# A hybrid layer kernel on one core: four edits of order, at its head, in the first steps of its mixer and at the mixer's end

## The reference, cut to what matters

```python
def _layernorm(x, axis=-1, eps=1e-05):
    m = jnp.mean(x, axis=axis, keepdims=True)
    v = jnp.var(x, axis=axis, keepdims=True)
    return (x - m) / jnp.sqrt(v + eps)

x = x + (block-masked linear layer 512 -> 512 with bias)(_layernorm(x))
x = x + ffn(_layernorm(x))      # 4-bit weights with group scales, 512 -> 1792 -> 512
x = x + mixer(_layernorm(x))
x = x + ffn(_layernorm(x))      # the same weights again

# the mixer (a selective state space layer; 128 heads of 64 channels, chunks of 128 tokens)
proj = hidden_states @ in_proj_w.T            # gate z, then x, B, C (8 groups of 128), then dt
hBC = silu(causal depthwise convolution with 4 taps of [x, B, C] + conv_b)
dt = softplus(dt + dt_bias); A_dt = -exp(A_log) * dt
Y_diag = einsum('bclsh,bcshp->bclhp', (C B^T) * exp(segment sums of A_dt), x * dt)
Y_off  = einsum('bclhn,bchpn->bclhp', C, carried states) * exp(cumulated A_dt)
y = Y_diag + Y_off + D * x
y = y * rsqrt(mean(y^2) + eps) * norm_w * silu(gate)
return y @ out_proj_w.T
```

## Time and profile before

| | |
|---|---|
| median of 3 runs | 2114.71 us (2114.70 to 2115.32) |
| the profiled execution: its time | 2115.85 us |
| the profiled execution: its span in the trace | 2114.1 us |
| busy: PE, DVE, ACT, POOL | 2067.3, 1656.5, 1424.1, 887.6 us |
| DMA, share of 16 engines | 44.4% |

### The profile page before, as it was taken

How to read it: one execution, slowest core, us unless ns; L and a number is a source line. 1 busy time by engine, 2 the same in 40 slices (tenths; PEclk the granted TensorE clock), 3 DMA queues, 4 the chain that set the end, 5 groups by cost and what they waited for, 6 DMA issues and landing times.

```text
span 2114.1 us, 35693 instructions
## 1 busy us (share of the span) xinstructions
PE 2067.3 (98%) x12366; PEld 1703.4 (81%) x12366; DVE 1656.5 (78%) x2676; ACT 1424.1 (67%) x2690; POOL 887.6 (42%) x616
## 2 busy tenths in 40 slices
PE   7999998999999999999999999999999999989999
PEld 6788876788888888888888888888888888878887
DVE  7655557888888888888888888888888888876554
ACT  4322268878787878778787877877877878742221
POOL 1221214445454545454454544454545555422121
PEclk9999999999999999999999999999999999999999
DMA  5543225445444444444444444445444444455341
GB/s 204 176 139 136 78 85 184 151 140 158 147 138 154 139 154 148 150 160 133 142 156 150 144 155 134 150 154 162 139 155 140 154 149 145 148 172 172 131 147 40
DMA packets 160095, 307.06 MB, mean 145 GB/s; under 512 B 14528, under 2 KB 47552, under 8 KB 159680
## 3 DMA queue, kind: packets, MB, share of 16 engines
q1 hardware_dynamic: 159936, 305.00, 44.4%
HBM read 299.70 MB, written 5.24 MB: 144 GB/s over the span
## 4 chain that ended last, share of the span: by engine, by line
PE 78%; DVE 10%; issue 5%; ACT 4%; POOL 1%; DMA 1%; DVEq 0%; ACTq 0%; SPq 0%; POOLq 0%
PE ring L1016 30%; PE ring L1104 14%; PE bank L410 6%; PE bank_e L410 6%; PE yt L1085 5%; PE st L1069 4%; PE bank_e L422 3%; PE yt L1091 3%; PE bank L422 3%; PE xt L1056 3%; DVE xc L1458 1%; DVE ce L1511 1%; DVE em L1519 1%; DVE ygs L1538 1%; DVE bc L1458 1%
## 5 line engine op out<-in xcount | busy, mean ns | idle before, releaser
L1016 PE MATMUL ring<-m_lnt,w_sb 128*128 128x512 f32 x3456 | 858.9, 398 | 5.5 <-ACT sz L1265 2.5
L1016 PEld LDWEIGHTS ring<-m_lnt,w_sb 128*128 128x128 f32 x3456 | 630.1, 188 | 134.0 <-issue 3.1
L1688 POOL TENSOR_TENSOR w_sb<-w_raw,w_sb 128x512 fp32r<-128x512 f32 x288 | 428.4, 1490 | 162.3 <-ACT w_sb L1243 162.0
L1705 POOL TENSOR_TENSOR ysq<-ysq,y 128x512 f32<-128x512 f32 x126 | 169.8, 1348 | 637.2 <-ACT y L1299 637.2
L1104 PE MATMUL ring<-wo,ygs 128*128 128x512 f32 x1536 | 372.2, 392 | 5.6 <-DVE ygs L1538 3.3
L1104 PEld LDWEIGHTS ring<-wo,ygs 128*128 128x128 f32 x1536 | 289.2, 189 | 68.0 <-issue 7.8
L1458 DVE SCALAR_TENSOR_TENSOR xc<-ring,cw,xc 128x511 f32<-128x511 f32 (+2 forms) x384 | 286.8, 747 | 52.3 <-ACT xc L1255 43.2
L1285 ACT ACTIVATE cum_b<-cum_b,cum_q 128x128 f32<-128x128 f32 x1024 | 312.5, 390 | 0.0
L1243 ACT ACTIVATE w_sb<-w_raw 128x512 fp32r<-128x512 f32 x288 | 178.2, 620 | 48.0 <-DMA w_raw<-w_in 47.8
L1693 POOL TENSOR_TENSOR wo<-wo_raw,wo 128x512 fp32r<-128x512 f32 x128 | 191.1, 1493 | 1.6 <-ACT wo L1311 1.6
L1085 PE MATMUL yt<-em,x_dt 128*64 128x128 f32 x2048 | 183.9, 279 | 3.6 <-DVE state L1499 3.5
(11 more groups left out here) (198 smaller groups left out, 2891.9 us busy)
## 6 DMA issues: line engine op xcount, KB each, us to landing
w_raw<-w_in SPq DMA_DIRECT2D x288, 256.0 KB, 3.4
cum_b<-c_t SPq DMA_DIRECT2D x128, 512.0 KB, 4.6
ce<-e_t SPq DMA_DIRECT2D x128, 384.0 KB, 4.5
wo_raw<-w_out SPq DMA_DIRECT2D x128, 256.0 KB, 3.0
f_gu_q<-gu_w SPq DMA_DIRECT2D x28, 512.0 KB, 3.5
f_gu_zr<-gu_z SPq DMA_DIRECT2D x28, 512.0 KB, 4.3
f_gu_sr<-gu_s SPq DMA_DIRECT2D x28, 512.0 KB, 5.3
f_dn_q<-dn_w SPq DMA_DIRECT2D x28, 256.0 KB, 3.4
```

The costliest lines, as they stand in the source:

```text
L1016: mm = nc.tensor.matmul(dst[:], w_sb[:, u % WR, wp, k * P:(k + 1) * P], lnt[:, xp, k, b * S:(b + 1) * S], start=(i == 0), stop=(i == 3 * K ...
L1688: nc.gpsimd.tensor_tensor(w_sb[:, u % WR, 1], w_raw[:, u % NR], w_sb[:, u % WR, 0].bitcast(F32), ALU.subtract).then_inc(w_lo, 1)
```

## The change

The rows of instructions below are those of the built programs; names are the program's tiles, and a row's x2 or x4 counts equal instructions in a row. Line numbers behind L1096 are higher in the changed kernel (by 4 to 9).

The fourth edit is on PE, at `project_out(31, 0)`: its first nine matmuls (pairs 124 to 126) wait for 127 low parts of the gated output and of the output weights, and the last three for all 128. The whole diff:

```diff
--- before.py
+++ after.py
@@ -611,8 +611,8 @@
                 nc.scalar.activation(share[:], ones[:], ACT.Copy, scale=1.0 / P).then_inc(self.hi, 1)
                 norm_root(act, na, 0)
                 center(na, 0)
+                norm_root(act, na, 1)
                 high(na, 0)
-                norm_root(act, na, 1)
                 center(na, 1)
                 high_w(0)
                 high_w(1)
@@ -1097,10 +1097,14 @@
                 def project_out(i, t):
                     dst = ring_bank(("out", (i, t)))
                     ring_free(("out", (i, t)))
-                    pe.wait_ge(yg_lo, HALF * (i + 1))
-                    pe.wait_ge(wo_lo, HALF * (i + 1))
+                    early = 1 if (i, t) == (K // HALF - 1, 0) else 0
+                    pe.wait_ge(yg_lo, HALF * (i + 1) - early)
+                    pe.wait_ge(wo_lo, HALF * (i + 1) - early)
                     for m, (j, (yp, wp)) in enumerate((j, ab) for j in range(HALF * i, HALF * (i + 1))
                                                       for ab in PASSES):
+                        if early and m == 3 * (HALF - 1):
+                            pe.wait_ge(yg_lo, K)
+                            pe.wait_ge(wo_lo, K)
                         mm = nc.tensor.matmul(dst[:], ygs[:, j % OR, yp, t * P:(t + 1) * P], wo[:, j % WOR, wp],
                                               start=(m == 0), stop=(m == 3 * HALF - 1))
                     mm.then_inc(out_mm, 1)
@@ -1411,6 +1415,8 @@
                     if k + 1 < K:
                         if k % 2:
                             exponent(k + 1)
+                        if k == 3:
+                            tap(("b", 1))
                         activate_x(k + 1)
                         activate_z(k + 1)
                     if 1 <= k <= K:
@@ -1419,7 +1425,8 @@
                     for unit in ahead[2:]:
                         w_high(unit)
                     for unit in bc_units(k):
-                        tap(unit)
+                        if k != 3:
+                            tap(unit)
                     for g in silu_in(k):
                         activate_bc(g)
                     if k + 1 < K and k % 2 == 0:
@@ -1623,7 +1630,7 @@
                             norm_shift(dve, n, i)
                     if k == K + 2:
                         factor_mean(1)
-                    if 2 <= k <= K + 1:
+                    if HALF < k <= K + 1:
                         y_low(k - 2)
                     if k == K + 1:
                         scale_gu(0, 0)
@@ -1667,6 +1674,8 @@
                         carry(k)
                     if k == 0:
                         conv(("x", 2))
+                    if 2 <= k <= HALF:
+                        y_low(k - 2)
                     if k == K - 1:
                         sub_gu(0, 0)
                     for g in gram_in(k):
```

## The result

| | median | runs |
|---|---|---|
| before | 2114.93 us | 20, 2112.54 to 2117.79 |
| changed | 2117.68 us | 20, 2116.03 to 2120.28 |

The ratio is 1.0013, 95% interval 1.0007 to 1.0019: +2.7 us, where the forecast was 2114.7 and the range ended at 2117.3. It lies within the 0.2% that was called no change, but it is a loss beyond its interval. Single runs of one kernel scatter by 4 to 5 us.

A forecast was written before the change was run, and what follows sets the result against it. PE, busy 98%, was taken to bound the kernel, with only its idle time at three places movable. Terms -1.3 + 1.05 + 0.3 = +0.05 us, taken as 2114.7 + 0.0, gave 2114.7 us, range 2111.8 to 2117.3.

The forecast's parts named there:

- The term of steps 2 to 4: Mixer's first steps: moved low parts stall ACT, tap of b gives part back; +1.05 us, bounds -1.1 and +4.6.
- The chain: Mixer steps 2 to 4: ACT's wait for y_low(0) passed through DVE, PE and POOL to tile (0, 0), 1.05 us late.
- The head's term: Head: the root runs 1.34 us sooner, so mix(0) starts at 16.2; -1.3 us, bounds -0.6 and -3.
- The bound of -0.7: Head: a clock that rises at the same moment whatever PE does would halve the term to -0.7 us.
- The end's term: Mixer's end: nine matmuls run early, but the clock falls soon and comes back soon after 1868.0; +0.3 us.
- rival N: Mixer's end: the clock stays up, end term -1.4, sum -1.7 us, 2113.0 us; chance 0.24.
- cases from -1.4 to +0.8: Mixer's end, last 36 matmuls: clock stays up -1.4 us, falls soon and recovers -0.4, falls there +0.8.
- S: Mixer's start: stall of activate_z in steps 2 and 4 not recovered, +4.6; sum +4.1 us, 2118.8 us; chance 0.07.
- M: Mixer's start gains because the wait at (0, 0) doesn't bind; 2110.9 to 2112.6 us; chance 0.08.
- W: Head gives nothing because the mask waits for its transfer anyway; +1.4 us, 2116.1 us; chance 0.09 with other such losses.
- What was taken as simply handed on: Outside head, mixer's start and end: a shift is handed on, since DVE, ACT and POOL follow PE.

The follow-up runs named there:

- e4: Changed kernel plus 14 useless filler matmuls in PE's pause before output tile (0, 0): 2114.87 us, ratio to before 0.9998.
- e5: Kernel before with only the root at the head moved: 2113.99 us, ratio 0.9995 (0.9986 to 1.0004).
- e6: Kernel before with only the nine early matmuls of output tile (31, 0): 2115.19 us, ratio 1.0003.
- e2: Kernel before with only the low parts of steps 2 to 4 moved: 2119.21 us, ratio 1.0022.
- e1: Changed kernel with the low parts put back at the head of steps 2 to 4: 2115.14 us, ratio to before 1.0000.
- e14: Changed kernel, low parts back at the head, early matmuls also at tile (0, 0), tile (31, 1) ahead of the transposes: 2111.38 us, ratio to before 0.9980.
- e7: Kernel before with only the tap of b in step 3 put ahead of the silus: 2114.87 us, ratio 0.9995.

## Why the prediction was wrong

1. **The term of steps 2 to 4 was mis-sized, and this decides.** It was put at +1.05 us; the trace shows 69.53 - 66.40 = +3.1. The chain itself held: ACT's wait of 4.52 us (forecast 4.6), PE's of 1.70 at `states(3)` (1.9), no wait for the tap of b, `activate_z(5)` at 375.06 with the head's shift in it. Tile (0, 0) started 0.75 us late, 1.5 without the head's shift, for 1.05. What failed is the last step, "from there PE has its backlog and hands on 1.05 us", which put the clock at nothing there: PE's pause before the tile had grown to 4.00 us, the clock fell, and the tile took 1.6 us longer. I had priced exactly this at the mixer's end and had all rows for it, and did not ask it where my own chain put a pause as long. e4 shows it: filler alone takes the median from 2117.68 to 2114.87. The prediction allowed for moved low parts that POOL slows down; here all three took 0.68 us, so nothing was added by that.
2. **The head's term** was -1.3 us and held: about -1.2 over all traces and -1.0 in the medians (e5), though the medians' interval takes in zero. The -0.8 of the changed kernel's own trace is scatter. The bound of -0.7, a clock that rises at the same moment whatever PE does, isn't what the traces show: starting 1.25 us sooner on average (16.25 for 17.50), `mix(0)` took no longer.
3. **The end's term** was +0.3 us. The profiled execution gained 1.05, against a slow sample; over all traces the edit costs 0.6, and the medians show +0.2 (e6). The clock in the new pauses is what the rows show, in each of the seven traces with the edit and no filling there, so rival N is out as the usual case. That the number agrees so well is partly luck: it was chosen between cases from -1.4 to +0.8.
4. **Rivals.** S named the right edit and the right sign. Its mechanism (the stall of step 4 isn't recovered) is not what happened, since the tap's move recovered most of it, but e2, without that move, shows it near its price: +4.3 us for the forecast 4.6. M is out: the wait at tile (0, 0) bound. W is out: the weights were there.
5. **What was taken as simply handed on** is so only to about a microsecond. From `states(5)` to the transposes of tiles 0 and 1 it takes 1472.5 us before and 1472.7 in the changed kernel, but 1472.0 to 1474.0 over all traces. The three terms of the trace, -0.8 + 3.1 - 1.05, give +1.25 of the 1.5 us between the spans. The medians differ by 2.75; with e5's -1.0 and e6's +0.2 they leave +3.5 for the start, near the 3.1 of its trace.

## What to carry to other kernels

A pause of PE costs its length and, at times, the pace of the matmuls behind it; so when an edit shifts a wait, price the clock at every pause that the new order makes, not only at the one the edit aims at. An edit that moves a producer later must be checked against every wait on its semaphore, here a buffer's reuse three steps on, not only against its reader. Filling a pause can pay even with useless work, as e4 shows. Useful work does it too: nine matmuls taken early at one tile and one tile taken ahead of a waiting transpose took the kernel from 2115.14 us (e1) to 2111.38 (e14). And the trace of one execution can have the other sign than the medians, as at the end: an edit worth a microsecond needs many runs and several traces.

## What the runs showed of the hardware

Idle time before tile (0, 0) and the pace behind it: behind pauses of 1.03 to 1.64 and of 2.49 us the twelve matmuls took 2.97 to 3.00 us; behind 2.90 us once 3.01 (e1) and once 4.58 (e7); behind 3.96 to 4.00 us 4.57, 4.57 and 5.46. The same instructions at the same place can thus fall on either side. Short waits don't rule a fall out: behind one of 2.04 us z of pair 2 took 4.57 us in the changed kernel, in e5 it took 2.98 behind 2.46; in e14 twelve matmuls took 4.60 us with waits of 1.06 and 0.19 us ahead of them. Fourteen useless matmuls in the pause of 4 us made the kernel 2.8 us faster. A fall of the clock is free where PE would have waited right behind it, as at z of pair 2. And at the head the twelve matmuls of `mix(0)` took anything from 4.41 to 5.46 us, with an early start or without.
